# Four layers of graph networks: two transposes taken from TensorE and given to VectorE's 32x32 blocks and SyncE's transfers

## The reference

```python
# layer 0, T=3 steps on h = x
a = adj @ h;  av = concat([a, a])
z = sigmoid(av @ w3.T + w3_b + h @ u3.T + u3_b)
r = sigmoid(av @ w4.T + w4_b + h @ u3.T + u3_b)
hv = tanh(av @ w5.T + w5_b + (r * h) @ u5.T + u5_b)
h = (1 - z) * h + z * hv
x = layernorm(x + h)
# layer 1
q, k, v = x @ Wq.T, x @ Wk.T, x @ Wv.T
rel = adj.T * (q @ k.T);  rel = rel / norm(rel, axis=2)
x = layernorm(x + rel @ v)
# layer 2 and layer 3
x = layernorm(x + (adj @ x) @ w2 + b2)
x = layernorm(x + norm_adj @ (x @ w3) + b3)     # norm_adj = adj / sqrt(deg deg')
```

## Time and profile before

| | |
|---|---|
| median of 3 runs | 1271.95 us (1271.56 to 1273.86) |
| profiled execution | 1271.8 us |
| its span | 1270.0 us |
| PE busy | 1240.6 us (98%), 7664 matmuls |
| PEld (weight loads) busy | 1103.3 us (87%) |
| DVE busy | 1031.4 us (81%) |
| ACT busy | 583.7 us (46%) |
| POOL busy | 192.4 us (15%) |
| DMA engines | mean 30 GB/s |
| mean granted TensorE clock | 0.995 |

### The profile page before, as it was taken

How to read it: one execution, slowest core, us unless ns; L and a number is a source line. 1 busy time by engine, 2 the same in 40 slices (tenths; PEclk the granted TensorE clock), 3 DMA queues, 4 the chain that set the end, 5 groups by cost and what they waited for, 6 DMA issues and landing times.

```text
span 1270.0 us, 21112 instructions
## 1 busy us (share of the span) xinstructions
PE 1240.6 (98%) x7664; PEld 1103.3 (87%) x7664; DVE 1031.4 (81%) x2274; ACT 583.7 (46%) x1007; POOL 192.4 (15%) x366
## 2 busy tenths in 40 slices
PE   7799999999999999999999999999999999999996
PEld 6589899898988989899898988989889898998895
DVE  5668889788888878888788888878888788895898
ACT  4444444444444444454444444444454445444442
POOL 0001112020210202112020110202112021110023
PEclk9999999999999999999999999999999999999999
DMA  7020110202001020010202002020010202000000
GB/s 199 1 50 1 38 30 1 66 0 59 7 17 50 0 66 0 33 33 0 66 0 50 17 17 50 0 66 0 21 45 0 66 0 49 17 17 18 1 1 34
DMA packets 86168, 37.56 MB, mean 30 GB/s; under 512 B 64768, under 2 KB 83200, under 8 KB 86144
## 3 DMA queue, kind: packets, MB, share of 16 engines
q1 hardware_dynamic: 84592, 36.71, 10.6%
q0 software_dynamic: 192, 0.52, 0.2%
q10 hardware_dynamic: 1360, 0.01, 0.1%
HBM read 20.45 MB, written 8.39 MB: 23 GB/s over the span
## 4 chain that ended last, share of the span: by engine, by line
PE 94%; DVE 4%; DMA 1%; POOL 1%; issue 0%; ACT 0%; ACTq 0%; DVEq 0%
PE b_ps L430 46%; PE f_ps L430 43%; PE f_ps L525 2%; PE b_ps L525 1%; DMA bias_in<-in_L_gnn_u_b 1%; PE b_ps L571 1%; DVE f_stats L1251 0%; DVE hf_feat L1267 0%; DVE normed L1267 0%; POOL f_rstd L364 0%; DVE f_cand L1184 0%; DVE b_stats L1251 0%; DVE f_kept L1178 0%; ACTq L827 0%; DVE f_a_lo L1162 0%
## 5 line engine op out<-in xcount | busy, mean ns | idle before, releaser
L362 POOL TENSOR_TENSOR b_var_eps<-b_moments,eps 128x2 f32<-128x2 f32 x120 | 44.1, 368 | 827.6 <-DVE b_moments L1258 827.6
L364 POOL TENSOR_TENSOR b_rstd<-b_var_eps,neg_half 128x2 f32<-128x2 f32 x120 | 97.0, 808 | 9.4
L866 ACT ACTIVATE f_z<-f_ps,bias_z 128x512 f32<-128x512 f32 x66 | 45.2, 685 | 92.5 <-PE f_ps L430 92.5
L870 ACT ACTIVATE f_cand<-f_ps,bias_c 128x512 f32<-128x512 f32 x66 | 45.5, 690 | 85.1 <-PE f_ps L430 85.1
L1168 DVE TENSOR_TENSOR f_gate<-f_gate,hf_feat 128x512 f32<-128x512 f32 x66 | 45.2, 685 | 46.2 <-ACT f_gate L858 46.0
L1251 DVE BATCH_NORM_STATS2 b_stats<-b_ps 128x6 f32<-128x256 f32 x180 | 68.3, 421 | 13.9 <-PE b_ps L430 13.3
L430 PE MATMUL f_ps<-adjT_hi,hf_node_hi 128*128 128x256 f32 x264 | 74.6, 283 | 0.0
L430 PE MATMUL f_ps<-adjT_hi,hf_node_lo 128*128 128x256 f32 x264 | 74.3, 282 | 0.0
L430 PE MATMUL f_ps<-adjT_lo,hf_node_hi 128*128 128x256 f32 x264 | 74.2, 281 | 0.0
L1290 DVE TENSOR_TENSOR b_rh_lo<-b_ps,b_rh_hi 128x512 fp32r<-128x512 f32 x90 | 61.9, 688 | 13.7 <-ACT b_rh_hi L824 13.4
L824 ACT ACTIVATE f_a_hi<-f_ps 128x512 fp32r<-128x512 f32 x66 | 39.0, 593 | 71.8 <-PE f_ps L430 71.8
(11 more groups left out here) (325 smaller groups left out, 4610.5 us busy)
## 6 DMA issues: line engine op xcount, KB each, us to landing
x_front<-in_x SPq DMA_DIRECT2D x16, 512.0 KB, 3.5
x_blocks<-in_x SPq DMA_DIRECT2D x60, 128.0 KB, 3.4
input_t<-hf_feat SPq DMA_DIRECT2D x15, 512.0 KB, 2.9
out<-result SPq DMA_DIRECT2D x15, 512.0 KB, 3.0
b_cand<-in_L_gnn_u_w SPq DMA_DIRECT2D x2, 256.0 KB, 8.9
bias_out<-in_L_gnn_bias POOLq DMA_DIRECT2D x4, 128.0 KB, 6.3
b_z<-in_L_gnn_w_w SPq DMA_DIRECT2D x1, 512.0 KB, 11.4
b_gate<-in_L_gnn_w_w SPq DMA_DIRECT2D x1, 512.0 KB, 12.4
```

Source lines behind the costliest of these rows:

```text
L364: pool.tensor_tensor(Y.rstd[:, g], Y.var_eps[:, g], neg_half[:], ALU.pow).then_inc(Y.s_rstd, 1)
L866: act.activation(L.z[:, k], L.ps0[:, k], ACT.Sigmoid, bias=bias_z[:, k:k + 1]).then_inc(L.s_z, 1)
L870: act.activation(L.cand[:, k], L.ps1[:, k], ACT.Tanh, bias=bias_c[:, k:k + 1]).then_inc(L.s_tanh, 1)
```

## The change

1. The front state after step 1: DVE turns the 32x32 blocks where they are (`turn_state`), SP moves 16 blocks of 32 partitions x 1 KB to their place (`move_blocks`, 16 transfers within SBUF), and ACT and DVE read the moved tile (`moved_hi`, `moved_lo`). `turn_h(state_f, ..)` is gone from `body`. The blocks use the tiles `f_gate` and `f_z`, free at that time.
2. The residual sum likewise: `turn_sum_blocks`, `move_sum` (16 transfers), through the tiles `normed` and `result`. Statistics and normalisation read `result` in SBUF.
3. 1/variance goes onto the values (`values_hi` by ACT's scale, `values_lo`), and the mask becomes one product with adj. The squares take `rstd` as their scale instead of `std`, which POOL no longer makes. `values` doesn't wait for the normalisation.
4. `body` is reordered on PE, ACT, DVE and POOL. `turn_h(state_b, ..)` stays, and so does the order in `finish`, which still turns on PE.

```diff
@@ SP: new functions, and their place in the loop
+            def move_blocks(S, turn):
+                sp.wait_ge(S.s_blocks, 2 * turn)
+                for a in range(4):
+                    for b in range(4):
+                        sp.dma_start(S.moved[32 * a:32 * a + 32, b],
+                                     S.blocks[32 * b:32 * b + 32, a]).then_inc(S.s_moved, 16)
+            def move_sum(Y, q):
+                sp.wait_ge(Y.s_sum_blocks, upto(q))
...
                 load_blocks(p + 1)
                 keep_input(p)
+                move_sum(main, p - 1)
+                move_blocks(state_f, p)
                 store(main, p - 1)
@@ PE: body
+                mix(front, 2 * p, 0, p)
                 for k in range(2):
                     reset(back, q, k)
...
-                reset(front, 2 * p, 0)
-                turn_sum(main, q, 0)
-                reset(front, 2 * p, 1)
-                turn_sum(main, q, 1)
...
                 candidate_mixed(front, 2 * p, 1)
                 candidate_reset(front, 2 * p, 1)
+                for k in range(2):
+                    keys(main, q, k)
                 values(main, q, 0)
+                relate(main, q, 0)
+                values(main, q, 1)
                 relate(main, q, 1)
-                for k in range(2):
-                    turn_h(state_f, 2 * p + 1, k)
-                values(main, q, 1)
+                base(front, 2 * p + 1, 0)
                 sum_squares(main, q, 0)
+                base(front, 2 * p + 1, 1)
                 attend(main, q, 0)
-                mix(front, 2 * p + 1, 0)
+                for k in range(2):
+                    mix(front, 2 * p + 1, k)
                 sum_squares(main, q, 1)
                 attend(main, q, 1)
...
                 mix_nodes(main, q, 0, 1)
+                for k in range(2):
+                    convolve(main, q, 0, k)
@@ ACT
+            def moved_hi(S, v, g, turn):
+                act.wait_ge(S.s_moved, 256 * turn)
...
             def values_hi(Y, q, g):
-                graph_hi(Y.v_hi, Y.ps1[:, g], Y.s_v, upto(q, g), g, Y.s_v_hi)
+                act.wait_ge(Y.s_v, upto(q, g))
+                act.wait_ge(Y.s_inv_var, upto(q, g))
+                for c in range(C):
+                    last = act.activation(Y.v_hi[:, g, c], Y.ps1[:, g, c * D:(c + 1) * D], ACT.Copy,
+                                          scale=Y.inv_var[:, g, c:c + 1])
@@ DVE
+            def turn_state(S, v, c):
+                dve.wait_ge(S.s_feat, upto(v, c))
+                out = S.blocks.rearrange("p q (u c i) -> p u q c i", c=C, i=32)[:, :, :, c]
+                dve.transpose(out, S.feat[:, c].rearrange("p (u q i) -> p u q i", q=4, i=32)).then_inc(S.s_blocks, 1)
+            def turn_sum_blocks(Y, q, c):
...
             def mask(Y, q, g):
                 dve.wait_ge(Y.s_rel, upto(q, g))
-                dve.wait_ge(Y.s_inv_var, upto(q, g))
-                for c in range(C):
-                    last = dve.scalar_tensor_tensor(Y.rel[:, g, c], Y.ps0[:, g, c * N:(c + 1) * N],
-                                                    Y.inv_var[:, g, c:c + 1], adj_nat[:, c], ALU.mult, ALU.mult)
+                dve.tensor_tensor(Y.rel[:, g], graph_bank(Y.ps0, g), adj_nat[:], ALU.mult).then_inc(Y.s_masked, 1)
```

More of the change, by code:

```diff
@@ L220, in per_graph, with quarters @@
             return t[:].rearrange("p c (k n) -> p c k n", k=C)
+        def quarters(t):
+            return t[:].rearrange("p c (u n) -> p (c u) n", u=2)
+        state_f.blocks, state_f.moved = quarters(front.gate), quarters(front.z)
         w3s_in = sb("w3s_in", [P, C, D])
@@ L625, in body @@
                 candidate_mixed(front, 2 * p, 0)
-                keys(main, q, 0)
-                update(front, 2 * p, 1)
                 candidate_reset(front, 2 * p, 0)
-                relate(main, q, 0)
-                keys(main, q, 1)
                 candidate_mixed(front, 2 * p, 1)
                 candidate_reset(front, 2 * p, 1)
+                for k in range(2):
+                    keys(main, q, k)
                 values(main, q, 0)
+                relate(main, q, 0)
+                values(main, q, 1)
@@ L642, in body @@
                 attend(main, q, 1)
-                mix(front, 2 * p + 1, 1)
                 for k in range(2):
-                    base(front, 2 * p + 1, k)
-                reset(front, 2 * p + 1, 0)
+                    reset(front, 2 * p + 1, k)
+                candidate_mixed(front, 2 * p + 1, 0)
                 mix_nodes(main, q, 0, 0)
-                reset(front, 2 * p + 1, 1)
+                update(front, 2 * p + 1, 0)
                 mix_nodes(main, q, 0, 1)
-                convolve(main, q, 0, 0)
@@ L651, in body @@
-                candidate_mixed(front, 2 * p + 1, 0)
-                convolve(main, q, 0, 1)
-                update(front, 2 * p + 1, 0)
+                for k in range(2):
+                    convolve(main, q, 0, k)
+                update(front, 2 * p + 1, 1)
                 candidate_reset(front, 2 * p + 1, 0)
-                update(front, 2 * p + 1, 1)
                 candidate_mixed(front, 2 * p + 1, 1)
@@ L882, in node_hi @@
                 copy(S.node_hi[:, g].rearrange("p c d -> p (c d)"), front.ps1[:, g]).then_inc(S.s_node_hi, 1)
+            def moved_hi(S, v, g, turn):
+                act.wait_ge(S.s_moved, 256 * turn)
+                if S is state_b and later(v):
+                    act.wait_ge(back.s_mixed, upto(v - 1))
+                rows = S.moved[:, :, g * P:(g + 1) * P].rearrange("p q (u i) -> p u q i", i=32)
+                copy(S.node_hi[:, g].rearrange("p h (c q i) -> p (h c) q i", q=4, i=32), rows).then_inc(S.s_node_hi, 1)
             def graph_hi(dst, src, ready, count, g, done):
@@ L948, in body @@
[L948 to L952, removed]
+                for k in range(2):
+                    rh_hi(front, 2 * p, k)
+                for k in range(2):
+                    update_gate(front, 2 * p, k)
+                for k in range(2):
+                    candidate(front, 2 * p, k)
@@ L961, in body @@
                 conv_ax_hi(main, q, 0, 0)
-                for k in range(2):
-                    reset_gate(front, 2 * p + 1, k)
+                reset_gate(front, 2 * p + 1, 1)
+                update_gate(front, 2 * p + 1, 0)
                 rh_hi(front, 2 * p + 1, 0)
@@ L1236, in input_lo, with moved_rows @@
                 feat_lo(state_f, 2 * p, k)
+            def turn_sum_blocks(Y, q, c):
+                dve.wait_ge(Y.s_sum_t, upto(q, c))
+                if later(q):
+                    dve.wait_ge(s_stored, 16 * q)
+                out = Y.sum_blocks.rearrange("p q (u c i) -> p u q c i", c=C, i=32)[:, :, :, c]
+                dve.transpose(out, Y.sum_t[:, c].rearrange("p (u q i) -> p u q i", q=4, i=32)).then_inc(Y.s_sum_blocks, 1)
+            def moved_rows(Y, g, c):
+                at = 64 * (C * g + c)
+                return Y.sum_moved[:, :, at:at + 64]
             def layer_sum(Y, j, g, c):
@@ L1250, in stats_of @@
                 for c in range(C):
-                    last = dve.bn_stats(Y.stats[:, g, c], layer_sum(Y, j, g, c))
+                    src = layer_sum(Y, j, g, c) if j or turned else moved_rows(Y, g, c)
+                    last = dve.bn_stats(Y.stats[:, g, c], src)
                 last.then_inc(Y.s_stats, 1)
```

236 lines of the change are left out of this document (131 added, 105 removed).

## The result

The changed kernel takes 1358.86 us (median of 4 runs, 1356.02 to 1363.38) against 1272.86 for the kernel before on the same chip (1271.56 to 1273.86): a ratio of 1.068, 95% interval 1.0647 to 1.0712. It is slower by 86 us. The forecast was 1256; what came is rival C, and beyond its upper end.

What follows compares the result with a forecast made beforehand. PE was taken as the bound, busy all 76.50 us of a pass. Transposes removed, 1.75, less waits of 0.4 and 0.2, gave 1.15 per pass, 16 us over 14 passes: 1271.8 to 1256, range 1247 to 1290.

Steps and rivals of the forecast that it cites:

- rival C: SP's issuing becomes the bound and the kernel slower, from 0.50 us per issue; 1315 us at 0.59; chance 0.20.
- the price of one issue, p: SP's time per transfer in each chain of 16: taken as 0.44 us, bounds 0.07 and 0.59.
- The landing: Time from a small transfer's issue to its arrival: put at 1.5 us, upper bound 2.9.
- The walk through the pass: Step-by-step timing of one pass: state's transfers hidden up to 0.42 us per issue, sum's to 0.47; `mix` waits 0.4.
- What was taken away and added on the engines: Per pass, 1.75 us of transposes off PE; DVE gains 2.3, to 65.9 us, hidden under PE.
- rival D: DVE late, not SP: scattered block transposes take twice 0.705, keys' rest 0.8 late at `relate`; 1267 us, chance 0.08.
- The second `convolve`: On PE, one unit behind its `mix_nodes` while the way over ACT and DVE takes 1.6: 0.2 us lost per pass.
- B's full gain: Rival with all transfers hidden: 1.55 us gained per pass, 1250 us, or 1247 without the 0.2 loss; chance 0.32.
- The estimate of 1263: Time if a transfer's fixed 2.0 us replaces 1.5, making the wait at `mix` 0.5 longer.

Runs made afterwards that it cites:

- 12 issues: Changed kernel with each chain's 16 SP transfers made into 12 (4 of 64 rows, 8 of 32; values not the reference's): 1277.1 us, 1.0038 of before.
- the shared version: Changed kernel with each chain's 16 transfers split 8 and 8 between SP and GpSimd, both moments_of directly behind stats_of: 1266.16 us, 0.9946 of before.
- 14 issues: Changed kernel with each chain's 16 SP transfers made into 14 (2 of 64 rows, 12 of 32; values not the reference's): 1317.38 us, 1.0347 of before.
- state 8: Changed kernel with only the state's chain cut to 8 transfers of 64 rows, the sum's kept at 16 (values not the reference's): 1304.21 us, 1.0247 of before.
- the first shared kernel: Changed kernel with GpSimd issuing 8 of the sum's 16 transfers and 6 of the state's, SP the rest: 1292.77 us, 1.0161 of before.
- sum 8: Changed kernel with only the sum's chain cut to 8 transfers of 64 rows, the state's kept at 16 (values not the reference's): 1349.39 us, 1.0597 of before.

## Why the prediction was wrong

**The step that failed is the price of one issue, p.** I took 0.44, the 0.39 of a load of 512 KB from memory and a gap of 0.05, because the rows hardly followed the amount. They don't; but the only copy within SBUF had taken 0.54, the transfers in question are within SBUF, and I made that row my upper end instead of my figure. The price measured 0.59 + 0.04 = 0.63, above even that end of 0.59. Why an issue within SBUF costs SP more than a load was not parted. The 0.84 of each `x_blocks` issue stood above that end too, as a sign that small pieces aren't cheaper. The landing, put at 1.5, measured 1.86 and added 0.4 to each chain. Together 8.1 us became 11.3.

**The walk through the pass held.** I gave the sum room up to p = 0.47, which is 15 x 0.47 + 1.5 = 8.6 us, and the state up to 0.42, 7.8 us. With 12 issues (8.8) `relate` doesn't wait and `mix` waits 0.87, so the room measured is 7.9 for the state and at least 8.8 for the sum. The places were right too: PE at `mix` and `relate`, DVE's statistics on the transfer. Rival C (both chains late, so 30p) gave the mechanism at a chance of 0.20; its range of p was too low by the same row. Two of its figures are not what its own working gives: with 15p - 6.25 for the state and 15p - 7.05 for the sum the waits at 0.50 and 0.59 are 1.7 and 4.4, and the time at 0.59 is 1312, not 1315. With the measured 0.63 and 1.86 the same form gives waits of 6.3 us and 1271.8 + 14 x (6.3 + 0.2 - 1.75) = 1338 us. So the price of the chains is the larger part of the loss: 66 of the 84 us between the two spans.

**What was taken away and added on the engines held, but for 0.7 us.** 1.75 us per pass off PE, DVE at 65.5 for 65.9, block transposes at 0.71 with the scattered output for 0.705, which ends rival D. The second `convolve` stalls 0.34 for 0.2; the 0.45 at the second `mix_nodes` was not foreseen. The pass without long waits is 75.64, where the prediction has 74.95. B's full gain was never there: with no long wait at all the kernel takes 1261, not 1250.

**A smaller term was missing:** the clock behind a wait. The account of a usual pass: 75.64 without long waits, 2.37 at `relate` and 1.97 at `mix` (both counted on PE's starts), and 1.7 left for the spell at half clock, together 81.7. The spell's net price is less, since without it the wait at `mix` would be longer: next to nothing in these passes and some 6.5 us in the four longer ones together, by the estimate above. Over the span: the first store comes 10.4 us later than before, 13 passes add 5.66 each on average, 73.6 us, and the end 0.2; that is the 84.2 between the two spans, 1354.2 and 1270.0. The first pass, with two spells, is in the 10.4, which I have not split further.

Of the two rules that I had weighed, the Trainium skill's "DMA: Bandwidth & Descriptors" with its fixed 2.0 us for a transfer, which its section "Anatomy of one DMA — SWDGE (gpsimd) path" fits on transfers issued by GpSimd, was nearer to the 1.86 measured on SP than my 1.5. The estimate of 1263 made with it fell with mine, since the issues and not the landings made the chain. The advice of the Trainium skill's "VectorE: DVE Perf Modes", Rules for kernel authors, to leave a full 128x128 transpose to TensorE where a PSUM destination will do, agrees with the kernel as it was changed; the shared version beats it by 0.5%, less than a third of the 24.5 us of transposes.

## What to carry to other kernels

Count the transfers that one queue must issue in a row, and price one by the nearest kind (within SBUF or from memory, pieces alike), not by its size; take its row as the middle of the range and not as its end, and compare the chain with the slack of the step that waits. Where it doesn't fit, share the issues with another queue, but put them where nothing of that engine is waited for. Where a wait of 2 to 3 us comes into a loop that TensorE bounds, read the granted clock behind it, and count what it costs only where no later wait would have hidden it.

## What the runs showed of the hardware

- An issue within SBUF on SP takes 0.63 us from start to start with 32, 64 or 128 rows (10.07 for 16, 5.00 for 8, 2.47 for 4), where the store of 512 KB takes 0.40 in the same queue. GpSimd's takes 0.50 (3.98 for 8), and the two queues run beside each other.
- The granted clock was at its lower level, 1.2 GHz, for some 3.4 us behind a wait in all 14 passes of the changed kernel (waits of 1.8 to 3.3 us, two per pass), in 6 of 13 with 14 issues (0.93 and 2.04 by the same view), in 3 of 14 with one wait of 2.2 to 2.9 us per pass (state 8), and in none with one of 0.8 (12 issues) or 1.5 (the first shared kernel). With one wait of 3.2 us and no other (sum 8) the spell was 6.8 us long in each pass. So the length of a wait alone doesn't tell whether the clock falls; what does was not parted.
- Moving work of PE to fill two small stalls (0.8 us per pass) brought a new one of 3.0 us, and in 12 of 14 passes a spell at the lower clock with it.
